# A selective scan and two attentions: passes by image, three units' state sums together, and work moved from VectorE to ScalarE and GpSimd

## The reference

```python
def selective_scan(xs, dts, As, Bs, Cs, Dsk):      # over the 256 tokens, 4 directions k, 96 channels c
    def step(h, inp):                              # h: 16 states n for each channel
        dA = jnp.exp(d_t[..., None] * As)
        h = h * dA + (d_t * u_t)[..., None] * B_t[:, :, None, :]
        y = jnp.einsum('bkcn,bkn->bkc', h, C_t)
...
xz = group_norm(x) @ in_proj_w.T                   # split into xh and z, 96 channels each
xc = silu(conv3x3_depthwise(xh) + conv_b)
x_hwwh = stack([rows of xc, columns of xc]);  xs = concatenate([x_hwwh, flip(x_hwwh)])   # 4 directions
dts, Bs, Cs = split(xs @ x_proj_w);  dts = softplus(dts @ dt_projs_w + dt_projs_b)
y = out_y[0] + flip(out_y[2]) + transposed(out_y[1]) + transposed(flip(out_y[3]))
x = x + (layernorm(y) * g + b) * silu(z) @ out_proj_w.T
# block 2: relu attention, 12 heads of 16, 64 features
qp = relu(q @ projection.T) + 1e-3;  kp = relu(k @ projection.T) + 1e-3
out = (qp @ (kp.T @ v)) / (qp @ kp.sum(tokens));   x = x + out @ w_proj.T + b_proj
# block 3, on t = layernorm(x): router keeps the top 6 of 12 heads, softmax attention of those
x = x + layernorm(softmax(q k / 4) v @ Wo + bo + t) * ln_g + ln_b
```

## Time and profile before

| | |
|---|---|
| median of three runs | 463.25 us |
| profiled execution | 463.01 us, its span 461.3 us |
| granted TensorE clock, mean | 0.891 |
| TensorE matmul | 371.3 us busy, 80% |
| TensorE weight load | 214.3 us, 46% |
| VectorE | 346.4 us, 75% |
| ScalarE | 179.8 us, 39% |
| GpSimd | 206.9 us, 45% |
| DMA | 12.69 MB, mean 28 GB/s |

### The profile page before, as it was taken

How to read it: one execution, slowest core, us unless ns; L and a number is a source line. 1 busy time by engine, 2 the same in 40 slices (tenths; PEclk the granted TensorE clock), 3 DMA queues, 4 the chain that set the end, 5 groups by cost and what they waited for, 6 DMA issues and landing times. The chain is left out here.

```text
span 461.3 us, 5553 instructions
## 1 busy us (share of the span) xinstructions
PE 371.3 (80%) x1669; PEld 214.3 (46%) x1669; DVE 346.4 (75%) x622; ACT 179.8 (39%) x405; POOL 206.9 (45%) x210
## 2 busy tenths in 40 slices
PE   5825499697887867857999998896989999969691
PEld 4612133142332312323557555553865786958450
DVE  5885989878999999999789898987457356263514
ACT  2565354554563534423243332335225211135340
POOL 7131697867895967774653863451121010000001
PEclk9999889979897987785999999999799989588966
DMA  5502212011121110110101010000000000000000
GB/s 121 106 21 64 56 26 64 23 41 34 23 58 34 47 40 18 40 43 9 47 21 33 11 34 1 0 2 1 2 17 1 1 0 17 2 1 1 1 17 18
DMA packets 15743, 12.69 MB, mean 28 GB/s; under 512 B 7279, under 2 KB 11361, under 8 KB 15713
## 3 DMA queue, kind: packets, MB, share of 16 engines
q1 hardware_dynamic: 15713, 12.33, 11.7%
HBM read 2.62 MB, written 0.79 MB: 7 GB/s over the span
## 5 line engine op out<-in xcount | busy, mean ns | idle before, releaser
L559 POOL TENSOR_TENSOR outp<-state,c_rep 128x512 f32<-128x512 f32 x96 | 126.4, 1321 | 93.0 <-PE y_acc L1397 43.1
L1019 DVE TENSOR_TENSOR_SCAN state<-decay,inp_bc 128x512 f32<-128x512 f32 x96 | 117.2, 1221 | 9.3 <-DVE inp_bc L1010 4.3
L1397 PE MATMUL y_acc<-outp,band 128*96 128x512 f32 x192 | 111.2, 666 | 6.7 <-DVE y_sum L1034 2.6
L732 ACT ACTIVATE decay<-step_bc,a_neg 128x510 f32<-128x510 f32 x96 | 64.9, 683 | 47.0 <-PE step_bc L1384 46.8
L1010 DVE TENSOR_TENSOR inp_bc<-b_rep,inp_bc 128x512 f32<-128x512 f32 x96 | 65.5, 682 | 7.1 <-PE inp_bc L1388 6.9
L1388 PE MATMUL inp_bc<-room_s,spread 96*128 96x512 bf16 x96 | 41.0, 427 | 31.1 <-DVE state L1019 31.0
L494 POOL TENSOR_TENSOR rs<-mv,neg_half 128x2 f32<-128x2 f32 x16 | 11.1, 696 | 120.0 <-DVE mv L1055 119.9
L1384 PE MATMUL step_bc<-room_s,spread 96*128 96x512 bf16 x96 | 39.9, 415 | 12.7 <-DMA room_s<-lo 11.6
L1397 PEld LDWEIGHTS y_acc<-outp,band 128*96 128x96 f32 x192 | 34.3, 182 | 24.7 <-issue 10.3
L1388 PEld LDWEIGHTS inp_bc<-room_s,spread 96*128 96x128 bf16 x96 | 9.9, 103 | 65.9 <-DVE state L1019 56.8
L1384 PEld LDWEIGHTS step_bc<-room_s,spread 96*128 96x128 bf16 x96 | 10.4, 109 | 32.5 <-issue 27.3
(11 more groups left out here) (346 smaller groups left out, 650.8 us busy)
## 6 DMA issues: line engine op xcount, KB each, us to landing
b_rep<-bc SPq DMA_DIRECT2D x64, 32.0 KB, 1.9
c_rep<-bc SPq DMA_DIRECT2D x64, 32.0 KB, 2.0
room_s<-hi SPq DMA_DIRECT2D x24, 64.0 KB, 2.0
room_s<-mid SPq DMA_DIRECT2D x24, 64.0 KB, 2.0
room_s<-lo SPq DMA_DIRECT2D x24, 64.0 KB, 2.0
x_tok<-in_x_dram SPq DMA_DIRECT2D x2, 384.0 KB, 3.8
out_dram<-room_g SPq DMA_DIRECT2D x4, 192.0 KB, 2.0
room_a<-in_L_attn_w_qkv_dram SPq DMA_DIRECT2D x1, 432.0 KB, 6.5
```

Of the source, the lines that this page charges most:

```text
L559: g.tensor_tensor(outp[:, u % SLOTS, :], state[:, u % STATE_SLOTS, :], c_rep[:, n % 2, :], ALU.mult).then_inc(S["outp"], 1)
L732: a.activation(decay[:, u % SLOTS, :, 1:L], step_bc[u % 2][:, :].rearrange("p (b l) -> p b l", b=IMG)[:, :, 1:L], ACT.Exp, scale=a_neg[:, ...
L1019: v.tensor_tensor_scan(state[:, u % STATE_SLOTS, :], decay[:, u % SLOTS, :, :].rearrange("p b l -> p (b l)"), inp_bc[u % 2][:, :], 0.0, AL ...
L1397: t_.matmul(y_acc[0:DI, :], band[:, at:at + DI], outp[:, u % SLOTS, :], start=(g12 == 0), stop=(g12 == UNITS - 1)).then_inc(S["y_mm"], 1)
```

## The change

A pass is now one image in two directions: forward by rows and by columns, or the same two backward. A backward pass reads the same data, and its scan runs through the three operands in reverse. A unit is 16 channels x 8 states of one of the two halves of the states (`part`), still 128 x 512, and there are still 8 passes of 12 units. Step and input rows are written to DRAM once a pass (`step_rows`), and for each unit a DMA reads its 16 rows, each into 8 partitions (`in_rep`, four slots of 128 x 1024 float32, 512 KB). C goes through DRAM too. B is made by TensorE with repeated weights (`fill_b`), two banks a pass. There is one bank `drv` for the product, and the product waits until the scan before is done. The decay is two instructions of 255 and has two slots for each direction sense. TensorE sums the states of three units in a row, which go to three groups of 32 output rows. In the head only image 0 is convolved on VectorE. All four images may have steps beside units, image 0 from unit 28; 64 steps are left for `rest`: none of image 0, 6 of image 1 (from `t0` on), 25 of image 2 (from `q2`), 33 of image 3. Queries and keys are taken off by ScalarE (Relu) and get their 1e-3 from GpSimd; two normalisations run on ScalarE with a shift that GpSimd makes; GpSimd adds the other eps and makes the input product.

```diff
-HALVES = 2
+WAYS = 2
+SN = 8
-RING = 3
-SLOTS = 3
+RING = 4
+SLOTS = 6
+IN_SLOTS = 4
+DECAY_SLOTS = 2
+BATCH = CHUNKS
-Y_LAG = 3
+Y_LAG = 4
...
-HEAD_STEPS = ["s0", "t0", "s1", "w0", "t1", "w1"]
+HEAD_STEPS = ["s0", "t0", "s1", "t1", "w"]
...
-        step_bc = [ctx.enter_context(nc.psum_tensor(f"step_bc{i}", [P, TOK], F32)) for i in range(2)]
-        inp_bc = [ctx.enter_context(nc.psum_tensor(f"inp_bc{i}", [P, TOK], F32)) for i in range(2)]
+        step_rows = nc.dram_tensor("step_rows", [2, DI, 2 * TOK], F32, kind="Internal").ap()
+        b_bc = [ctx.enter_context(nc.psum_tensor(f"b_bc{i}", [P, TOK], F32)) for i in range(PARTS)]
+        drv = ctx.enter_context(nc.psum_tensor("drv", [P, TOK], F32))
...
+            def repeat_step(u):
+                _, _, _, g = unit(u)
+                n = u // UNITS
+                if u % UNITS == 0:
+                    sp.wait_ge(S["step_kept"], 16 * (n + 1))
+                if u >= IN_SLOTS:
+                    sp.wait_ge(S["decay"], u - IN_SLOTS + 1)
+                    sp.wait_ge(S["drive"], u - IN_SLOTS + 1)
+                rows = step_rows[n % 2, GRP * g:GRP * (g + 1), :]
+                sp.dma_start(in_rep[:, u % IN_SLOTS, :, :].rearrange("p a t -> p (a t)"),
+                             rows.unsqueeze(1).to_broadcast([GRP, SN, 2 * TOK])).then_inc(S["in_there"][u % IN_SLOTS], 16)
...
+            def pre_inp(n):
+                pool.wait_ge(S["sp_max"], n + 1)
+                pool.wait_ge(S["xs"], n // PER_IMAGE + 1)
+                g.tensor_tensor(step2[0:DI, 1, :], step2[0:DI, 0, :], xs[:, n // PER_IMAGE, :, :].rearrange("p e l -> p (e l)"),
+                                ALU.mult).then_inc(S["step"], 1)
...
+                        g.tensor_scalar(mv[:, at, ts, 1], mv[:, at, ts, 1], eps, None, ALU.add).then_inc(S["eps_" + tag], 1)
                         inv_sqrt(rs[:, at, ts], mv[:, at, ts, 1], "eps_" + tag, n + 1, "rsqrt_" + tag)
+                        if tag in "tu":
+                            g.tensor_scalar(mv[:, at, ts, 0], mv[:, at, ts, 0], -1.0, None, ALU.mult).then_inc(S["neg_" + tag], 1)
...
+                            g.tensor_tensor(mv[:, at, ts, 0], mv[:, at, ts, 0], rs[:, at, ts], ALU.mult).then_inc(S["shift_" + tag], 1)
...
+                kept = slice(0, L - 1) if back else slice(1, L)
+                for e in range(WAYS):
+                    at = (part * DIRS + WAYS * back + e) * GROUPS + c16
+                    ins = a.activation(decay[:, back, u % DECAY_SLOTS, e, kept],
+                                       in_rep[:, slot, 0, :].rearrange("p (e l) -> p e l", e=WAYS)[:, e, kept],
+                                       ACT.Exp, scale=a_neg[:, at:at + 1])
...
+                    for t in range(2):
+                        a.activation(dst[:, 2 * b + t, :], x_tok[:, 2 * n + t, :], ACT.Identity, bias=mv[:, at, 2 * b + t, 0:1],
+                                     scale=rs[:, at, 2 * b + t:2 * b + t + 1]).then_inc(S["norm_" + tag], 1)
+                elif step[0] == "q":
+                    a.activation(qp[:, i:i + 2, b * L:(b + 1) * L], bank(name)[:, :].rearrange("p (i l) -> p i l", i=2),
+                                 ACT.Relu).then_inc(freed(name), 1)
...
+                if u:
+                    dve.wait_ge(S["state"], u)
+                v.tensor_tensor(drv[:, :], in_rep[:, slot, 1, :], b_bc[part][:, :], ALU.mult).then_inc(S["drive"], 1)
...
+                back = unit(u)[1]
+                order = slice(None, None, -1) if back else slice(None)
+                held = decay[:, back, u % DECAY_SLOTS, :, :].rearrange("p e l -> p (e l)")
+                v.tensor_tensor_scan(state[:, u % STATE_SLOTS, :][:, order], held[:, order], drv[:, :][:, order],
+                                     0.0, ALU.mult, ALU.add).then_inc(S["state"], 1)
...
+            def sum_states(first):
...
+                pe.wait_ge(S["outp"], first + BATCH)
...
+                for u in range(first, first + BATCH):
+                    c16 = unit(u)[3]
+                    rows = slice(CHUNK * (c16 // PER_CHUNK), CHUNK * (c16 // PER_CHUNK + 1))
+                    at = CHUNK - GRP - GRP * (c16 % PER_CHUNK)
+                    t_.matmul(y_acc[rows, :], band[:, at:at + CHUNK], outp[:, u % SLOTS, :],
+                              start=(g == 0), stop=(g == PER_IMAGE * UNITS - BATCH)).then_inc(S["y_mm"], 1)
```

More of the change, by code:

```diff
@@ L120, in side_work @@
             ready[n] = u + UNITS_AFTER.get(step, UNITS_AFTER_ELSE)
-    at = {step: i for i, step in enumerate(steps)}
-    done += [0, 0]
     rest = []
@@ new lines, in _ @@
+            keep_c(0)
+            keep_step(0)
+            for u in range(2):
+                repeat_step(u)
+            for i in range(PARTS):
+                repeat_c(0, i)
+            for u in range(2, IN_SLOTS):
+                repeat_step(u)
+            for u in range(SLOT_COUNT):
+                n, at = u // UNITS + 1, u % UNITS
+                later = SECOND_LATER if n == 1 else 0
+                if n < SCANS and at == AT_ROWS + later:
+                    keep_c(n)
+                if n < SCANS and at == AT_STEP + later:
+                    keep_step(n)
+                if n < SCANS and at == AT_REPEAT[0]:
+                    repeat_c(n, 0)
+                if n > 1 and at == AT_REPEAT[1] - UNITS:
+                    repeat_c(n - 1, 1)
+                if u + IN_SLOTS < SLOT_COUNT:
+                    repeat_step(u + IN_SLOTS)
@@ L676, in weights @@
+            for n in range(1, IMAGES):
+                group_normed(n)
+            for n in range(1, IMAGES):
+                pad(n)
             def weights(step):
@@ new lines, in collected, with group_deviations @@
+            def collected(first, last, count):
+                dve.wait_ge(S["gn_stats"], count)
+                for s in range(2 * first, 2 * last):
+                    v.bn_aggr(gmv[:, s, :], gst[:, s, :]).then_inc(S["gn_agg"], 1)
+            def group_deviations(i, cols):
+                w = cols.stop - cols.start
+                fetched(dve, f"gm{i}")
+                dve.wait_ge(S["gn_agg"], cols.stop)
+                v.tensor_copy(gmean[:, cols], bank(f"gm{i}")[0:CK, 0:w]).then_inc(freed(f"gm{i}"), 1)
+                taken(dve, f"gm{i}")
+                v.tensor_tensor(gdv[:, cols], gmv[:, cols, 0], gmean[:, cols], ALU.subtract).then_inc(S["gn_dev"], 1)
+                dve.wait_ge(S["gn_dev"], 2 * i + 1)
+                v.tensor_tensor(gsq[:, cols], gdv[:, cols], gdv[:, cols], ALU.mult).then_inc(S["gn_dev"], 1)
+                dve.wait_ge(S["gn_dev"], 2 * i + 2)
+                v.tensor_tensor(gva[:, cols], gsq[:, cols], gmv[:, cols, 1], ALU.add).then_inc(S["gn_var"], 1)
@@ L910, in _ @@
+            one, others = slice(0, 2), slice(2, 8)
+            turned_stats(0, 0)
+            turned_stats(0, 1)
+            collected(0, 1, 2)
             v.memset(v1[:, :, :, HD:HD + 1], 1.0).then_inc(S["ones"], 1)
-            v.memset(cbd[:], 0.0).then_inc(S["ones"], 1)
             v.memset(rin[CK:CK + 1, :, :], float(L)).then_inc(S["ones"], 1)
+            group_deviations(0, one)
+            turned_stats(1, 0)
+            group_rsqrt(0, one)
+            turned_stats(1, 1)
+            turned_stats(2, 0)
@@ L913, in _ @@
+            group_bias(0, one)
+            turned_stats(2, 1)
+            for c in range(2):
+                turned_stats(3, c)
+            collected(1, IMAGES, 2 * IMAGES)
             for e in range(2):
@@ L915, in _ @@
                     v.memset(one_of[:, e, d, :], float(e == d)).then_inc(S["ones"], 1)
+            group_deviations(1, others)
+            v.memset(cbd[:], 0.0).then_inc(S["ones"], 1)
             dve.wait_ge(S["w_small"], 64)
@@ L1300, in _ @@
             done(ins)
[L1301 removed]
+            taken(pe, "w_in")
+            inner(0)
+            group_means(1, others)
+            group_vars(1, others)
             b_ = begin("w_alog")
[L1303 removed]
+            pe.wait_ge(S["w_alog"], 32)
             done(t_.transpose(b_[:, 0:DIRS * UNITS], alog[:], ident[0:DIRS * UNITS, 0:DIRS * UNITS]))
[L1305 to L1312 removed]
             b_ = begin("w_fold")
@@ new lines, in pre, with fill_b @@
+            def pre(n):
+                b_ = begin(f"d{n}")
+                for e in range(WAYS):
+                    ins = way(b_, n, e)
+                done(ins)
+            def fill_b(n, part):
+                if n:
+                    pe.wait_ge(S["drive"], UNITS * (n - 1) + GROUPS * (part + 1))
+                i = n // PER_IMAGE
+                pe.wait_ge(S["xs"], i + 1)
+                for e in range(WAYS):
+                    k = WAYS * (n % PER_IMAGE) + e
+                    ins = t_.matmul(b_bc[part][:, e * L:(e + 1) * L], w_b[:, k, part, :], xs[:, i, e, :], start=True, stop=True)
+                ins.then_inc(S["b_there"], 1)
@@ L1595, in side @@
                     done(ins)
-            front("z", 0)
+            for n in range(1, IMAGES):
+                inner(n)
             b_ = begin("d0")
```

885 lines of the change are left out of this document (373 added, 512 removed).

## The result

The changed kernel takes 479.17 us (median of four, 476.86 to 480.98), the kernel before beside it 462.47; the ratio is 1.0365 (95% interval 1.0299 to 1.0431). The forecast was 446 us with a range to 476: wrong in sign and outside the range. The profiled execution took 480.98 us with a span of 479.3. (Some executions of a kernel run longer at a lower clock throughout; ratios leave them out, so a ratio can be lower than its medians say, as in e7, and where few are left there is none.)

What follows compares the result with a forecast made beforehand. VectorE was taken to bound the scan stage, TensorE to be the busy engine in the tail. Head 41.5, stage 277.8 and tail 125.2 gave 444.5 us, with 1.7 around the span 446 us; range 424 to 476.

Steps and rivals of the forecast that it cites:

- TensorE's clock: Rival, chance 0.25: less TensorE work in the stage lowers its clock, products beside scans lengthen, 21 us, about 466 us.
- Waits in the stage: Scan stage: VectorE idle 29 us instead of 26.2, +2.8 us, from score, gate, query and value steps.
- GpSimd ... readers of its results are two units later, so 0.: Scan stage: work moved to GpSimd delays no reader, 0 us; without cover at most 0.70 us per small instruction.
- Removed from VectorE, -21.0: Scan stage: evictions, normalisations, eps additions, input products and image sums taken off VectorE, -21.0 us.
- The waiting product, +10.6: Scan stage: with one PSUM bank each product waits for the scan before it, 0.11 us x 96, +10.6 us.
- Feed, 0: Scan stage: reading 512 KB a unit through DRAM at 300 GB/s takes 1.75 us and is hidden, 0 us.
- Sums together: Scan stage: three units' state sums in three column groups cost about 0.9 us instead of 2.6 on TensorE.
- backward scans: Scan stage: scans running backwards through memory take no longer than forward ones, 0 us; at most a doubling, 59 us.
- Head, +0.5: Before the first scan: less convolution on VectorE against DRAM transfers and ScalarE's normalising and padding, +0.5 us, bounds -2 to +4.
- Tail, +6.5: After the last scan: image 3's first steps 1, normalisations across engines 2.5, value products 2, eps 1, +6.5 us.
- the equal part: Tail: the earlier trace from 346.3 us, where nearly the same steps remain, taken over as 115.0 us after 3.7 us.
- less waiting: Rival, chance 0.18: stage waits fall from 29 to 8 us and the tail's 6.5 us are hidden, 422 us.

Runs made afterwards that it cites:

- e7: Changed kernel with all moved work (queries, keys, eps, normalisations, input product) back on VectorE: 479.66 us, ratio 1.0266.
- e8: Changed kernel with queries and keys on VectorE, 512-column TensorE products added in light units and four before each context product: 467.51 us, ratio 1.0112.
- e2: Changed kernel with VectorE again taking queries and keys off their banks, GpSimd adding nothing to them: 479.02 us, ratio 1.0364.
- e9: Changed kernel with the same added TensorE products as e8, GpSimd's additions to queries and keys left in: 471.38 us.
- e14: e8 with two PSUM banks for the product, a ring of three, moved weight steps, and a 256-column product ahead of each step's product in the tail: 539.33 us.
- e5: Kernel before, with only queries and keys taken off by ScalarE (Relu) and GpSimd adding the 1e-3: 466.16 us, ratio 1.0085.
- e6: Kernel before, with only eps and shift of the normalisations on GpSimd and the plain normalisations on ScalarE: 463.29 us, ratio 1.0003.
- e16: e15 and in addition the input product of each pass on GpSimd: 456.22 us, ratio 0.9879.
- e15: Kernel before, with e6's edit only for images whose step lies beside units: 459.43 us, ratio 0.9937.
- e12: Changed kernel with two PSUM banks for the product, three ring banks instead of four, eight weight steps at other units: 481.93 us, ratio 1.0447.
- e3: Changed kernel with each unit's read bringing only step rows, 256 KB instead of 512 KB (computes something else): 475.87 us, ratio 1.0323.
- e11: e10 without the added TensorE products: 474.07 us, ratio 1.0298.
- e10: e8 with eps and plain normalisations on VectorE again for images whose step lies behind the last unit: 475.02 us, ratio 1.0229.
- e1: Changed kernel with one float32 TensorE product of 512 columns more in each of 84 of 96 units: 488.99 us, ratio 1.0595.
- e4: Changed kernel with every second unit's product written to SBUF, so the product waits only for the scan before the last: 503.11 us.

## Why the prediction was wrong

The span is 34.8 us above the sum: head +4.0, stage +16.7, tail +14.1. Step by step:

- **TensorE's clock.** This is the step that failed. The forecast's sum has no term for it: its waits of 29 us and its tail of 115.0 us are those of the clock of before, 0.90 and 0.83. It stood as a rival at 466 us with a chance of 0.25. The rival's mechanism was right: with the spreading products gone and three sums in six records of 1.06 us, the clock in the stage fell to 0.69 between its levels of 1.2 GHz (0.5) and 2.4. Its price was not: it was put on the stage alone, 21 us. The stage lost 7 to 8 us by it, and the tail, which had 0.76, another 7 (e8 against e2, e9 against the changed kernel), 14.5 us of the 34.8. The Trainium skill (TensorE: Matmul & The Clock Gate, Part 1) says that the default is the throttled clock and that activity releases it. The stage agrees (0.69 for 203.8 busy us in the changed kernel, 0.83 for 223.7 in e8); e14's tail does not, with 0.60 for 118 of 120 us, and the measurement decides.
- **"Waits in the stage ... I take 29 us."** Idle were 48.1. The 18.8 us at the context and attention products were not in the sum at all: I priced the query products by TensorE's time, and left the two steps whose results ScalarE and VectorE fetch in order before the next unit. At the high clock and without GpSimd they shrink from 18.8 to 5.9 us at these places in e8.
- **"GpSimd ... readers of its results are two units later, so 0."** Its additions take 1.2 and 1.5 us, not the 0.70 of the earlier trace rows, which I took as the bound; the context product is issued one unit after the last keys. That costs 6.6 us of idle time and 2.7 us of the stage (e9 against e8), about the same as at the low clock.
- **Removed from VectorE, -21.0.** VectorE's busy time in the stage came out near the sum, 246.4 us for 248.8, but the parts did not: queries and keys took 4.9 us off it in e5 where 7.5 were priced, and all the moved work 13.9 (e7). The time followed less still: in the kernel before the normalisations bring 4.5 of their 6.2 us, the input product 2.3 of 4.2, queries and keys 0.5 of 7.5 (e6, e16 against e15, e5).
- **The waiting product, +10.6.** Measured 0.20 us a unit instead of 0.11 where nothing else lies between, which would be 19 us over 96 units: a mis-sized term. No run gave more than 5.3 us back (e12). The gap after a scan is 0.10 us, not the 0.03 after a product.
- **Feed, 0.** Taken at 300 GB/s, 1.75 us a unit; measured 236 GB/s from 42 to 120 us, 2.2 us a unit, above the bare unit of 2.05. So the first pass was not covered; e3 gives 3 to 6 us.
- **Sums together** (six records in 1.06 us at the higher clock, 1.93 at the lower), **backward scans, decays** (a pair in 0.90 us): right.
- **Head, +0.5.** It was +4.5. In order of time, from the last input product to the first product of a unit:
```profile
35.95 0.69 DVE L1208 TENSOR_TENSOR step<-step,xs 96x512 f32<-96x512 f32 x1
36.67 0.31 SPq L455 DMA_DIRECT2D step_rows<-step  x1
39.66 1.25 SPq L467 DMA_DIRECT2D in_rep<-step_rows  x2
44.49 0.70 DVE L1021 TENSOR_TENSOR drv<-in_rep,b_bc 128x512 f32<-128x512 f32 x1 [7.85 <-DMA in_rep<-step_rows]
```
The write takes 3.0 us and the read 4.8, two others beside it; the input product itself is 2.3 us later than in the earlier trace rows, where it was to be no later. The head's own terms (5 us less, 3.5 and 1.0 more) add up to -0.5, not to the +0.5 that was taken.
- **Tail, +6.5.** It was +20.6 against the 118.7 us of the equal part. The clock is 7 of it (e8), the normalisations' way over GpSimd and ScalarE 5 (e11 against e2) instead of 2.5; no run here accounts for the rest.

Two of the rivals' sums don't come out as written either, which changes nothing in the above: less waiting takes off 3 us for a tail term of 6.5 that it says is hidden, and the clock's 21 us on 446 are 467, not 466.

What stays open: which work of TensorE counts for its clock, and hence why it was low in the tails of e10 and e14. Open too is why the changed kernel's tail had 0.76 where the equal part had 0.83: the change takes no product off TensorE there, and e1, which raised the stage's clock, left the tail's as it was. The shares above are not exact for that reason: each edit also moves the clock.

## What to carry to other kernels

When a change takes work off TensorE because it is "too busy", price what is left at both levels of the clock, in every stage and not only where the work goes: here the clock of the freed engine fell from 0.90 to 0.69. Before an operation moves to another engine, ask who stands in order behind its eviction, and what the relieved engine will wait for next; 4.9 us off VectorE's busy time were worth 0.5 in e5. Move work only where the giving engine is short: the same normalisations gain beside the scans and lose behind them. e15, which splits them so, is 0.6% faster than the kernel before, and e16, with the input product moved too, 1.2%.

## What the runs showed of the hardware

A scan whose inputs both lie in SBUF took up to 2.36 us beside GpSimd's weighing, and 1.22 with one input in PSUM, at any time (e4). The Trainium skill (SBUF — State Buffer, Who interferes with whom) says that a VectorE instruction with two SBUF inputs contends with a GpSimd instruction that reads SBUF; the trace agrees, with 1.14 us of standing for an instruction of 1.27. And TensorE's granted clock was 0.60 over 120 us in which its products were busy 118 (e14), and 0.61 over 20 us in which they were busy 19.98 (the changed kernel).
